# First layer of a two-layer attention kernel: the value product in four column quarters of 32 channels instead of two halves of 64

## The chip, the cores and the metric

The kernel runs on one core of one Trainium2 chip. The metric is the device time of one execution in microseconds (us), lower is better. TensorE (PE) does the matrix products, ScalarE (ACT) the exponentials and some copies, VectorE (DVE) maxima and small vector work, GpSimd (POOL) part of the sums, and SyncE (SP) starts the DMAs.

## The reference

Two self-attention layers over 8 images of 64x64 pixels with 64 channels, so 4096 tokens for each image. All is float32.

```
def layer0(x):                       # x: 8 images, xf = [8, 4096, 64]
    f, g, hh = xf @ wf + bf, xf @ wg + bg, xf @ wh + bh      # 8, 8 and 64 channels
    attn = softmax(einsum('bnk,bmk->bnm', g, f))
    return gamma * einsum('bnm,bmc->bnc', attn, hh) + x

def layer1(x):
    q, k, v = x @ Wq + bq, x @ Wk + bk, x @ Wv + bv          # 64 channels each
    attn = softmax(einsum('bic,bjc->bij', q, k))
    out = einsum('bmn,bmc->bnc', attn, v)                    # attention transposed
    return gamma * out + x
```

## The kernel before

The 8 images are worked one after the other, first layer and then second layer of each. What follows concerns the first layer.

The queries of an image are four chunks of 1024, and the keys are 32 tiles of 128. A chunk `q` is a loop of 32 steps `i` (`chunk0`), one for each key tile. The order on each engine is the order of the code; semaphores connect the engines. On TensorE a step is, in this order:

- `scores0` (L448): the scores of key tile `i` against the 1024 queries, as two matmuls of 512 columns in float16, with 34 of the 128 contraction rows. Between them stand two matmuls of the pass ahead (`max_pass_tiles`, L420), 33 contraction rows, which make scores of a later chunk only so that VectorE can take row maxima from them (`block_max`, L895). The L448 and L420 matmuls lie in different row groups of the array and all use its 128 columns.
- `values0` (L462), for the key tile four steps back (`LAG0`): it takes the exponentials `e_whole` (128 keys x 1024 queries, float32) and multiplies them with the value tile `proj[..., GFW:PW]` (128 keys x 64 channels). The 64 channels fill only half of the array's columns, so the first 512 queries go to columns 0 to 63 and the other 512 to columns 64 to 127. Both write bank 0 of `sum_banks`.
- `sum_of` (L484), every fourth step behind `values0`: it adds the exponentials over the keys for the softmax denominators. The other three of four key tiles are added up on GpSimd (`add_probs`, L346, L343) in `e_sum`. `sum_of` multiplies with a block of ones `ones_w` of 32 columns, in four column groups, each with its own quarter of 256 queries (`SUMS = 4`, `SQ = 256`), into bank 1.

ScalarE takes the exponential of each step's scores (L730), two steps behind at most. At the start of the next chunk the previous one is finished: values of its last four tiles in steps 0 to 3, `last_sums0` in step 4, VectorE's reciprocal of the sums (L900, `inv_d`), `spread0` (L494, two column groups of 64) in step 5, and VectorE's two products (L931, L932). The values of the new chunk are one step later than `LAG0` until step 8 (`CATCH_AT`), which does two value tiles, with a `sum_of` between them. Step 25 waits for VectorE's row maxima of the next chunk (L923), and step 26 (`MROW_AT`) transposes them (`max_rows`, L431, 34 columns) for ScalarE's copy L711, for which step 27 waits.

In the first chunk of an image (q = 0) there is no earlier chunk to finish, and values start in step 4. After the fourth chunk come the second layer's projections (L396) with the last value tiles between them.

The second layer's scores (L544) and values (L556) both use two column groups of 64 with all 128 rows.

A float32 matmul is two records in the trace, so 4096 records at L462 are 2048 matmuls, two for each of 1024 steps.

Of the kernel before, what the change touches and what calls it, by code (L numbers as in the profile page):

```python
# [24 lines left out]
P = 128  # L25
# [5 lines left out]
def attention_pair_kernel(nc, x, wf, bf, wg, bg, wh, bh, gamma0, wq, bq, wk, bk, wv, bv, gamma1, out):  # L31
    B, H, W, C = x.shape
# [13 lines left out]
    GFW = 2 * CK  # L46
    PW = GFW + C
# [20 lines left out]
    SUMS = 4  # L68
# [14 lines left out]
    with ExitStack() as ctx:  # L83
        def sb(name, shape, dt):
            return ctx.enter_context(nc.sbuf_tensor(name, shape, dt))
# [6 lines left out]
        sum_banks = ctx.enter_context(nc.psum_tensor("sum_banks", [P, 4, BANK], F32))  # L92
# [33 lines left out]
        proj = sb("proj", [P, 2, T, PW], F32)  # L126
# [77 lines left out]
        def on_pool(i):  # L204
            return i % GROUP != GROUP - 1
# [157 lines left out]
        def _(pe):  # L363
# [92 lines left out]
            def values0(image, par, q, i):  # L456

                pe.wait_ge(exp0_done, image * NCH * T + q * T + i + 1 + FREE_ST)
                if i == 0:
                    pe.wait_ge(v0_copied, image * NCH + q + FREE)  # L460
                for half in range(2):
                    mm = nc.tensor.matmul(sum_banks[half * C:(half + 1) * C, 0, :], proj[:, par, i, GFW:PW],  # L462
                                          e_whole[:, i % U0, half * BANK:(half + 1) * BANK], start=i == 0, stop=i == T - 1,
                                          skip_group_check=True)
                if i == T - 1:
                    mm.then_inc(v0_full, 1)
                    return
                if on_pool(i):
                    mm.then_inc(pv0_done, 1)
                    return  # L470
                if i == GROUP - 1:
                    pe.wait_ge(mid_ready, image * NCH + q + FREE)
                sum_of(e_whole[:, i % U0, :], i == GROUP - 1, False).then_inc(pv0_done, 1)
# [7 lines left out]
            def sum_of(terms, first, final):  # L481
                for c in range(SUMS):
                    rows = slice(c * (P // SUMS), (c + 1) * (P // SUMS))
                    mm = nc.tensor.matmul(sum_banks[rows, 1, 0:SQ], ones_w[:, :], terms[:, c * SQ:(c + 1) * SQ],  # L484
                                          start=first, stop=final, skip_group_check=True)
                return mm
# [16 lines left out]
            def chunk0(image, par, q):  # L503
# [5 lines left out]
                for i in range(T):  # L509
                    step = image * NCH * T + q * T + i  # L510
                    tiles = range(2 * (i % 4), 2 * (i % 4) + 2)
                    if q == 0 and i == 0:
                        pe.wait_ge(y_act, image * (NCH // 2) + FREE)
                        pe.wait_ge(y_dve, image * (NCH // 2) + FREE)
                    if i == MROW_AT + 1:
                        pe.wait_ge(mrow_sb, image * NCH + q + 2)
                    if i < LAST:
                        scores0(image, par, q, i, after(image, par, q + 1), EARLY + i // 4, tiles)
                    else:
                        scores0(image, par, q, i, after(image, par, q + 2), (i - LAST) // 4, tiles)  # L520
                    if i == MROW_AT:
                        max_rows(image, q)
                    if q == 0 or i > CATCH_AT:
                        if i >= LAG0:
                            values0(image, par, q, i - LAG0)
                    elif i < LAG0:
                        values0(image, par, q - 1, T - LAG0 + i)
                    elif i == LAG0:
                        last_sums0(image, q - 1)
                    else:  # L530
                        values0(image, par, q, i - LAG0 - DELAY)
                        if i == SPREAD_AT:
                            spread0(image, q - 1)
                        if i == CATCH_AT:
                            values0(image, par, q, i - LAG0)
# [608 lines left out]
```

## Time and profile before

| | |
|---|---|
| Median of 3 runs | 4095.75 us (4094.1 to 4095.97) |
| The profiled execution | 4098.83 us, its span 4097.0 us |
| PE busy | 3912.3 us (95%) |
| DVE busy | 3316.5 us (81%) |
| ACT busy | 2782.6 us (68%) |
| POOL busy | 1913.5 us (47%) |
| Mean granted TensorE clock | 0.979 |

The span is the time from the first to the last instruction. Busy shares are means over both layers. In the profile's lists "L462" is a line of the kernel, "out<-in" names what is written and read, "PE" are matmuls, "PEld" are weight loads, and "x4" counts the records. "128*64" is the part of the array that is used, rows times columns.

### The profile page before, as it was taken

The page shows a single profiled execution, that of the slowest core. Times are in us where ns is not written, and L with a number is a line of the kernel's source. Part 1 is how long each engine was busy: PE and PEld are TensorE (multiplying, and loading weights), DVE is VectorE, ACT ScalarE, POOL GpSimd, SP SyncE. Part 2 cuts the span into 40 slices and gives each one's busy share as a digit, 9 for nine tenths or more (in the row PEclk, how much of TensorE's full clock was granted, in tenths as well). Part 3 has the DMA queues.
Part 4 walks back from the last instruction along what each step waited for, and adds up shares of the span by engine and source line. Part 5 has one row for each costly group of instructions (what it writes and reads, how often), then busy time and mean ns, then how long its engine had stood idle before and what let it go on. Part 6 is the DMA issues. An engine that isn't in the chain of part 4 may idle for free.

```text
span 4097.0 us, 80148 instructions
## 1 busy us (share of the span) xinstructions
PE 3912.3 (95%) x25617; PEld 1432.4 (35%) x25617; DVE 3316.5 (81%) x6272; ACT 2782.6 (68%) x3610; POOL 1913.5 (47%) x876
## 2 busy tenths in 40 slices
PE   6999999999999999999999999999999999999999
PEld 3223442244422443224432244323442234422344
DVE  5777987788877888778877788777887779877798
ACT  1566776666766767666776667666676667766677
POOL 3695108931089311992039810497105961079410
PEclk8899999999999999999999999999999999999999
DMA  1000000000000000000000000000000000000000
GB/s 34 1 1 22 1 1 11 1 22 1 12 1 1 22 1 11 1 1 22 1 12 1 6 17 1 11 1 22 1 1 12 1 22 1 1 11 1 22 1 11
DMA packets 13900, 33.36 MB, mean 8 GB/s; under 512 B 3940, under 2 KB 3940, under 8 KB 12132
## 3 DMA queue, kind: packets, MB, share of 16 engines
q1 hardware_dynamic: 13540, 28.57, 2.4%
q8 instruction: 225, 3.69, 0.4%
q14 instruction: 135, 1.11, 0.1%
HBM read 11.78 MB, written 8.39 MB: 5 GB/s over the span
## 4 chain that ended last, share of the span: by engine, by line
PE 79%; DVE 11%; issue 7%; ACT 2%; DVEq 0%; SPq 0%; POOL 0%; DMA 0%; ACTq 0%; POOLq 0%
PE sum_banks L462 21%; PE score_banks L544 20%; PE sum_banks L556 19%; PE score_banks L448 11%; DVE tile_max L895 3%; PE sum_banks L484 3%; PE sum_banks L420 2%; DVE inv_d L900 1%; DVE e_whole L1062 1%; DVE c_stack L922 1%; PE sum_banks L494 1%; ACT g_tr L711 1%; DVE part_scr L1038 1%; PE score_banks L412 1%; DVE x_abs L876 0%
## 5 line engine op out<-in xcount | busy, mean ns | idle before, releaser
L895 DVE TENSOR_REDUCE tile_max<-sum_banks 128x1 f32<-128x512 f32 (+1 forms) x2128 | 1360.4, 684 | 474.1 <-PE sum_banks L420 471.7
L346 POOL TENSOR_TENSOR e_sum<-e_sum,e_whole 128x1024 f32<-128x1024 f32 x704 | 1660.1, 2358 | 129.9 <-ACT e_whole L730 82.1
L730 ACT ACTIVATE e_whole<-score_banks,no_bias,down 128x1024 f32<-128x1024 f32 x1024 | 1229.4, 1204 | 569.3 <-PE score_banks L448 532.6
L790 ACT ACTIVATE e_whole<-e_whole,exp_bias 128x1024 f32<-128x1024 f32 x1024 | 1176.2, 1149 | 514.9 <-DVE e_whole L1062 497.7
L1062 DVE TENSOR_SCALAR_CACHE_REDUCE e_whole<-score_banks,neg_down 128x1024 f32<-128x1024 f32 x1024 | 1293.6, 1281 | 121.8 <-PE score_banks L544 105.5
L462 PE MATMUL sum_banks<-e_whole,proj 128*64 128x512 f32 x4096 | 1122.5, 627 | 0.0
L556 PE MATMUL sum_banks<-e_whole,v_scaled 128*64 128x512 f32 x4096 | 1052.1, 594 | 40.1 <-DVE v_scaled L1051 29.0
L544 PE MATMUL score_banks<-k_high,q_split 128*64 128x512 f16 x4096 | 800.5, 381 | 12.3 <-DMA k_low<-k_low 9.7
L544 PE MATMUL score_banks<-k_low,q_split 128*64 128x512 f16 x4096 | 798.6, 380 | 0.0
L420 PE MATMUL sum_banks<-f_tr,g_tr 33*128 33x512 f16 x2128 | 700.0, 401 | 39.8 <-DVE tile_max L895 31.2
L448 PE MATMUL score_banks<-g_tr,f_tr 34*128 34x512 f16 x2048 | 648.3, 391 | 27.1 <-issue 11.2
L343 POOL TENSOR_TENSOR e_sum<-e_whole 128x1024 f32<-128x1024 f32 x32 | 75.4, 2356 | 1252.5 <-ACT e_whole L730 1252.5
L544 PEld LDWEIGHTS score_banks<-k_high,q_split 128*64 128x64 f16 x4096 | 244.7, 110 | 439.6 <-issue 169.9
L448 PEld LDWEIGHTS score_banks<-g_tr,f_tr 34*128 34x128 f16 x2048 | 123.2, 94 | 749.1 <-issue 596.8
L556 PEld LDWEIGHTS sum_banks<-e_whole,v_scaled 128*64 128x64 f32 x4096 | 299.2, 137 | 235.0 <-issue 43.4
L544 PEld LDWEIGHTS score_banks<-k_low,q_split 128*64 128x64 f16 x4096 | 246.5, 110 | 356.2 <-issue 250.3
L462 PEld LDWEIGHTS sum_banks<-e_whole,proj 128*64 128x64 f32 x4096 | 207.9, 136 | 303.9 <-issue 158.9
L420 PEld LDWEIGHTS sum_banks<-f_tr,g_tr 33*128 33x128 f16 x2128 | 177.5, 94 | 204.3 <-DVE tile_max L895 128.1
L790 ACT ACTIVATION_READ_ACCUMULATOR e_whole<-e_whole,exp_bias 128x1 f32 x1024 | 190.7, 186 | 0.0
L1051 DVE TENSOR_TENSOR v_scaled<-v,norm_w 128x256 f32<-128x256 f32 x256 | 115.2, 450 | 62.3 <-DVE norm_w L1042 60.1
L484 PE MATMUL sum_banks<-e_whole,ones_w 128*32 128x256 f32 x2048 | 164.5, 393 | 0.0
L317 POOL TENSOR_TENSOR f_stack<-fg_high,ones_h 128x512 f16<-128x512 f16 x20 | 20.9, 1062 | 253.4 <-issue 224.9
(128 smaller groups left out, 1735.5 us busy)
## 6 DMA issues: line engine op xcount, KB each, us to landing
x_in<-in_x_dram SPq DMA_DIRECT2D x11, 1024.0 KB, 5.1
out_dram<-y_out SPq DMA_DIRECT2D x32, 256.0 KB, 2.8
k_high<-k_high SPq DMA_DIRECT2D x32, 128.0 KB, 2.2
k_low<-k_low SPq DMA_DIRECT2D x32, 128.0 KB, 2.2
w<-in_L_conv_wg_dram SPq DMA_DIRECT2D x2, 2.0 KB
w<-in_L_conv_wf_dram SPq DMA_DIRECT2D x2, 2.0 KB
w<-in_L_conv_wh_dram SPq DMA_DIRECT2D x2, 16.0 KB
b<-in_L_conv_bh_dram SPq DMA_DIRECT2D x1, 32.0 KB
```

The costliest lines, as they stand in the source:

```text
L346: nc.gpsimd.tensor_tensor(acc, acc, e_whole[:, i % U0, :], ALU.add).then_inc(e_added, 1)
L420: nc.tensor.matmul(sum_banks[:, (2 + j % banks) % 4, :], g_tr[HIGH:KX, par, q * CH + blk * P:q * CH + (blk + 1) * P], f_tr[HIGH:KX, par, j ...
L448: mm = nc.tensor.matmul(score_banks[:, 2 * (i % 2) + h, :], f_tr[0:KM, par, i * P:(i + 1) * P], g_tr[0:KM, par, q * CH + h * BANK:q * CH + ...
L462: mm = nc.tensor.matmul(sum_banks[half * C:(half + 1) * C, 0, :], proj[:, par, i, GFW:PW], e_whole[:, i % U0, half * BANK:(half + 1) * BAN ...
L484: mm = nc.tensor.matmul(sum_banks[rows, 1, 0:SQ], ones_w[:, :], terms[:, c * SQ:(c + 1) * SQ], start=first, stop=final, skip_group_check=True)
L544: mm = nc.tensor.matmul(bank[c * C:(c + 1) * C, :], q_split[:, query_col(i) + c * C:query_col(i) + (c + 1) * C], k_part[:, col:col + BANK] ...
L556: mm = nc.tensor.matmul(sum_banks[half * C:(half + 1) * C, j, :], v_scaled[:, u // NCH, j, :], half_of_chunk(u, half), start=i == 0, stop= ...
L730: nc.scalar.activation(e_whole[:, i % U0, :].rearrange("p (a n) -> p a n", a=2), score_banks[:, 2 * (i % 2):2 * (i % 2) + 2, :], ACT.Exp, ...
L790: nc.scalar.activation(e_whole[:, u, :], e_whole[:, u, :], ACT.Exp, bias=exp_bias[:, u:u + 1], scale=-1.0, accum_out=part_sum[:, u // NCH, ...
L895: nc.vector.reduce_max(tile_max[:, blk, j:j + 1], sum_banks[:, (2 + j % banks) % 4, :], AX_X).then_inc(a_used, 1)
L1051: nc.vector.tensor_tensor(v_scaled[:, par, :, :], v1[:, i, :].unsqueeze(1).to_broadcast([P, NCH, C]), norm_w[:, par, :].unsqueeze(2).to_br ...
L1062: nc.vector.tensor_scalar(e_whole[:, u, :], score_banks[:, 2 * (u % 2):2 * (u % 2) + 2, :] .rearrange("p a n -> p (a n)"), neg_down[:, par ...
```

## The change

`values0` issues four matmuls instead of two. Each takes 32 of the 64 channels as its weights and one of the two query halves as its moving data: quarters 0 and 1 are the two channel halves for the first 512 queries, quarters 2 and 3 those for the other 512. They write the same elements of bank 0 as before. The division of the array into four column groups of 32 is the one that `sum_of` has. Streamed columns (512 each) and semaphores stay as they are.

```
@@ values0 @@
-                for half in range(2):
-                    mm = nc.tensor.matmul(sum_banks[half * C:(half + 1) * C, 0, :], proj[:, par, i, GFW:PW],
+                for c in range(SUMS):
+                    rows = slice(c * (P // SUMS), (c + 1) * (P // SUMS))
+                    half, part = c // 2, c % 2
+                    mm = nc.tensor.matmul(sum_banks[rows, 0, :],
+                                          proj[:, par, i, GFW + part * (C // 2):GFW + (part + 1) * (C // 2)],
                                           e_whole[:, i % U0, half * BANK:(half + 1) * BANK], start=i == 0, stop=i == T - 1,
                                           skip_group_check=True)
```

No instruction changes its place; lines behind L461 move down by 3 (L462 becomes L464, L484 becomes L487). Two places on TensorE show what now stands beside what. The first is the end of step 8 in a chunk after the first of its image (the values of tile 3, the sums, the values of tile 4). Before:

```order
L420 MATMUL sum_banks<-f_tr,g_tr 128x512
L462 MATMUL sum_banks<-e_whole,proj 64x512 x2
L484 MATMUL sum_banks<-e_whole,ones_w 32x256 x4
L462 MATMUL sum_banks<-e_whole,proj 64x512 x2
L446 REGISTER_ALU
```

The same rows of the changed kernel:

```order
L420 MATMUL sum_banks<-f_tr,g_tr 128x512
L464 MATMUL sum_banks<-e_whole,proj 32x512 x4
L487 MATMUL sum_banks<-e_whole,ones_w 32x256 x4
L464 MATMUL sum_banks<-e_whole,proj 32x512 x4
L446 REGISTER_ALU
```

The values now have the 32-column groups of the sums between them. The second place is step 5 of such a chunk, where `spread0` (64-column groups) follows the values. Before:

```order
L420 MATMUL sum_banks<-f_tr,g_tr 128x512
L462 MATMUL sum_banks<-e_whole,proj 64x512 x2
L494 MATMUL sum_banks<-inv_d,ident 64x256 x4
L446 REGISTER_ALU
L448 MATMUL score_banks<-g_tr,f_tr 128x512
```

And in the changed kernel:

```order
L420 MATMUL sum_banks<-f_tr,g_tr 128x512
L464 MATMUL sum_banks<-e_whole,proj 32x512 x4
L497 MATMUL sum_banks<-inv_d,ident 64x256 x4
L446 REGISTER_ALU
L448 MATMUL score_banks<-g_tr,f_tr 128x512
```

Here the two neighbours had the same column groups before and have different ones now.

## Rows read from the trace of the kernel before

**Rows 1.** The page: busy time, and the chain that ended last by line
```profile
PE 3912.3 (95%) x25617; PEld 1432.4 (35%) x25617; DVE 3316.5 (81%) x6272; ACT 2782.6 (68%) x3610; POOL 1913.5 (47%) x876
...
PE sum_banks L462 21%; PE score_banks L544 20%; PE sum_banks L556 19%; PE score_banks L448 11%; DVE tile_max L895 3%; PE sum_banks L484 3%; PE sum_banks L420 2%; DVE inv_d L900 1%; DVE e_whole L1062 1%; DVE c_stack L922 1%; PE sum_banks L494 1%; ACT g_tr L711 1%; DVE part_scr L1038 1%; PE score_banks L412 1%; DVE x_abs L876 0%
```

**Rows 2.** Timeline, PE, first layer, steps 15 to 17: start us, duration us
```profile
1266.34 1.08 PE L462 MATMUL sum_banks<-e_whole,proj 128*64 128x512 f32 x4
1267.34 0.64 PE L484 MATMUL sum_banks<-e_whole,ones_w 128*32 128x256 f32 x8
...
1267.92 0.39 PE L420 MATMUL sum_banks<-f_tr,g_tr 33*128 33x512 f16 x1
...
1268.45 1.08 PE L462 MATMUL sum_banks<-e_whole,proj 128*64 128x512 f32 x4
1269.46 0.39 PE L448 MATMUL score_banks<-g_tr,f_tr 34*128 34x512 f16 x1
...
1269.69 0.39 PE L420 MATMUL sum_banks<-f_tr,g_tr 33*128 33x512 f16 x1
```

**Rows 3.** Timeline, PE, second layer, where scores and values both have 64-column groups
```profile
1042.40 0.38 PE L544 MATMUL score_banks<-k_low,q_split 128*64 128x512 f16 x2
1042.62 1.02 PE L556 MATMUL sum_banks<-e_whole,v_scaled 128*64 128x512 f32 x4
1043.47 0.38 PE L544 MATMUL score_banks<-k_high,q_split 128*64 128x512 f16 x2
```

**Rows 4.** Groups by form, weight loads of one chunk: count, busy us, mean ns, idle
```profile
L462 PEld LDWEIGHTS sum_banks<-e_whole,proj 128*64 128x64 f32 x128 | 6.4, 134 | 8.8 <-ACT e_whole L730 4.7 <-issue 4.1
L484 PEld LDWEIGHTS sum_banks<-e_whole,ones_w 128*32 128x32 f32 x64 | 1.3, 108 | 5.9 <-issue 5.9
```

**Rows 5.** Timeline, PE, the first four records of one group of sums
```profile
1267.34 0.42 PE L484 MATMUL sum_banks<-e_whole,ones_w 128*32 128x256 f32 x4
```

**Rows 6.** Timeline, DVE, beside the steps of rows 2
```profile
1268.35 1.29 DVE L895 TENSOR_REDUCE tile_max<-sum_banks 128x1 f32<-128x512 f32 x2 [0.84 <-PE sum_banks L420]
```

**Rows 7.** Timeline, PE, step 8 of a chunk that finishes another
```profile
1253.01 0.39 PE L420 MATMUL sum_banks<-f_tr,g_tr 33*128 33x512 f16 x1 [0.21 <-DVE tile_max L895]
1253.33 1.08 PE L462 MATMUL sum_banks<-e_whole,proj 128*64 128x512 f32 x4
1254.34 0.64 PE L484 MATMUL sum_banks<-e_whole,ones_w 128*32 128x256 f32 x8
1254.90 1.08 PE L462 MATMUL sum_banks<-e_whole,proj 128*64 128x512 f32 x4
1255.92 0.39 PE L448 MATMUL score_banks<-g_tr,f_tr 34*128 34x512 f16 x1
```

**Rows 8.** Timeline, all engines, step 5 of that chunk
```profile
1246.29 1.08 PE L462 MATMUL sum_banks<-e_whole,proj 128*64 128x512 f32 x4
...
1247.69 1.08 PE L494 MATMUL sum_banks<-inv_d,ident 128*64 128x256 f32 x8 [0.32 <-DVE inv_d L900]
```

**Rows 9.** The waits, whole span: us in total, times, longest us
```profile
PEld sum_banks L494 <- DVE inv_d L900: 46.6, 32, 2.2
```

**Rows 10.** Timeline, all engines, steps 26 and 27
```profile
1286.01 0.57 PE L431 MATMUL score_banks<-ident_h,c_stack 128*34 128x128 f16 x7
...
1286.42 0.22 PE L431 MATMUL score_banks<-ident_h,c_stack 128*34 128x128 f16 x1
1286.47 1.02 PE L462 MATMUL sum_banks<-e_whole,proj 128*64 128x512 f32 x3
...
1287.73 0.39 PE L448 MATMUL score_banks<-g_tr,f_tr 34*128 34x512 f16 x1 [0.23 <-ACT g_tr L711]
```

**Rows 11.** Timeline, POOL, the first sum of the next chunk
```profile
1300.34 2.37 POOL L343 TENSOR_TENSOR e_sum<-e_whole 128x1024 f32<-128x1024 f32 x1 [0.64 <-ACT e_whole L730]
```

**Rows 12.** Windows, first chunks of two images: length, PE, PEld, DVE, ACT, POOL, PEclk
```profile
1116.60:1179.30 62.70, 60.77 (x306) 14.16 (x306) 43.30 (x67) 39.44 (x33) 51.72 (x22) 0.84 0.03 8
1616.20:1673.40 57.20, 54.85 (x304) 13.48 (x304) 43.09 (x67) 39.30 (x33) 51.28 (x22) 0.94 0.06 19
```

## The prediction

> **What bounds the kernel now.** The page comes first: TensorE is busy 95% of the span, and of the chain that ended last L462, the line that changes, holds 21% and its partner L484 3% [rows 1]. So a gain or loss of TensorE time at L462 can reach the end, if nothing else is equally late. The page can't say how long one value product occupies the array, since its records overlap. The timeline can, if one reads from the start of one group to the start of the next [rows 2]. The values take 1.01 us until the next scores start (1268.45 to 1269.46). Values with sums behind them take 1.58 (1266.34 to 1267.92), of which the sums are 0.58.
>
> How much of this is streaming? The second layer has values of the same size (four records, float32, 512 columns, groups of 64), between scores that use the same column groups. There it is 0.85 us from values to scores (1042.62 to 1043.47), and 0.22 from the last scores to the values: they follow each other without a gap [rows 3]. So 0.85 is the streaming, and 1.01 - 0.85 = 0.16 is lost in the first layer, where each neighbour divides the array otherwise: drain behind the group, and the first weight load, for which nothing runs as cover. The sums stream half as many columns, 0.43, and lose 0.58 - 0.43 = 0.15. The loss thus belongs to the change of division and not to the number of matmuls. By the Trainium skill (TensorEngine Tiling, Key Properties) changing the tiling mode drains TensorE while other tiles of the same mode run on; the rows agree, with 0.16 and 0.15 against nothing.
>
> **The change, part by part.**
>
> *Streaming.* The two quarters of a query half read the same exponentials, 512 columns each. All four must run at the same time, or the group doubles. The sums show four groups of 32 at once: eight records with a mean of about 0.4 in 0.58 [rows 2, 5]. The second layer shows two groups with the same moving data at once: two records in 0.22 (1042.40 to 1042.62) [rows 3]. I take 0.85 as before.
>
> *Starts and weight load.* In a group of sums the first four records span 0.42, one lasts some 0.40: three more starts cost 0.02 [rows 5]. The values would have two starts more, 0.014. A weight load of 32 columns has a mean of 108 ns against 134 for 64 [rows 4], so the exposed first one is 0.026 shorter. Together a value group between scores goes from 1.01 to 1.00: 0.012 saved. The loss of a 32-column group is then that of the sums, 0.15 instead of 0.16, as it should be.
>
> *Values and sums together.* They have the same division now, so I expect no loss between them: 0.85 + 0.43 + 0.15 = 1.43 instead of 1.58, 0.155 saved (with the third decimals of the means). Bounds: 0.012 if the gap between them stays, 0.155 if it goes.
>
> *Step 8.* Values, sums and values follow each other, 1253.33 to 1255.92, 2.59 us [rows 7]. New: 0.85 + 0.43 + 0.85 + 0.15 = 2.28, 0.31 saved.
>
> *New changes of division.* Two neighbours that agreed no longer do. `spread0` follows the values in step 5. The values end streaming near 1246.29 + 1.00 = 1247.29, drain included; L494 starts at 1247.69, because it waits for VectorE's reciprocal [rows 8]. So 0.40 covers it, and it waits so all 32 times [rows 9]. Without that cover it would cost 0.15 a time, 5 us in all. In step 26 the transposed maxima L431 use 34 columns of a 64-wide group and the values follow inside their stream; they would start about 0.13 later. The last pass starts near 1286.90, streams 0.43 and drains 0.10: 1287.43, or 1287.56 then. Step 27 waits until 1287.73 for ScalarE's copy [rows 10]. Hidden, at most 4 us if it were not.
>
> *What of it is on the path.* In chunks that finish another one, steps 5 to 7 lead through VectorE (reciprocal, two products, late maxima: L420 waits for them in step 8 [rows 7, 8]), step 24 through VectorE's maxima, step 26 through ScalarE's copy. Value time saved there is lost. The last four value tiles of an image lie beside ScalarE's and VectorE's work on the projections, before the same wait of L494 [rows 9]; I count nothing there. On the path remain: step 8 in 24 chunks; values with sums in six steps of those and seven of each first chunk, 24 x 6 + 8 x 7 = 200; values alone in 19 steps of those and 18 of each first chunk, 24 x 19 + 8 x 18 = 600.
>
> *VectorE is nearly as late.* Its two maxima start 0.43 after the first L420 of a step (1267.92 to 1268.35) and end 1.29 later, at 1269.64 [rows 2, 6]. The second L420 of the next step needs one of their banks and starts at 1269.69, 0.05 later, the time a semaphore takes, and its place in TensorE's own order is the same 1269.69 (0.23 behind the first) [rows 2]. So the two loops tie within 0.01. If values get 0.012 shorter, VectorE delays that L420 by 0.01 in every second step; the step after a delayed one has slack again. I give values alone 0.008 instead of 0.012, and values with sums 0.145 instead of 0.155. The sums' steps have slack on VectorE: it is idle 0.84 before the maxima there [rows 6].
>
> *GpSimd.* A chunk gets about 1.3 us shorter; GpSimd has 0.64 idle at its start [rows 11] and falls behind by under 1 us. Its last sum of a chunk ends at 1300.34 - 0.64 = 1299.70, before the exponential of the next chunk's step 1, and is wanted in step 4, three steps later; ScalarE needs the exponentials' slots only eight steps later. No cost.
>
> Sum: 24 x 0.31 = 7.4; 200 x 0.145 = 29.0; 600 x 0.008 = 4.8; together 41.2 us. The profiled execution would go from 4098.8 to 4057.6, its span from 4097.0 to 4055.8. It is 3.1 us above the median of the runs, so in medians: 4095.75 - 41.2 = 4054.5.
>
> *The clock.* TensorE starts an image's first chunk partly at 1.2 GHz, after little work: of two such chunks one has a mean granted clock of 0.84 and takes 62.7, the other 0.94 and 57.2 [rows 12]. How long it stays low differs from image to image, so a shift of everything in time deals these 5.5 us anew, eight times. I take 0 and allow 10 to both sides.
>
> **Rivals.**
>
> *A: the gap between values and sums stays* (because it comes from the other bank, the other weights or the last weight load, not from the division). Against it: in the second layer neighbours with other banks and other weights leave no gap [rows 3]. Then only 0.012 a group: 848 groups x 0.008 = 7, 4089.
>
> *B: VectorE or GpSimd takes more.* Both are near. If each plain step gives nothing and values with sums half, 7.4 + 200 x 0.08 = 23, 4072.
>
> *C, slower: four more records cost issue time in each group.* The nearest row is L431, where passes follow each other every (0.57 - 0.22) / 6 = 0.058 us [rows 10], though each also streams 128 columns, so it is an upper bound; the lower is the 0.007 from the starts [rows 5]. At 0.058, four more cost 0.23 in each of the 200 + 600 + 48 = 848 groups on the path: 196, minus 36 for the gaps, 4256. It decides from 36 / 848 = 0.043 a group, 0.011 a record. Against it: the sums issue eight records with the same 0.15 of loss as the values' four. The Trainium skill says (TensorEngine Tiling, Instruction Overhead) that each matmul has about 60 cycles of overhead. As an estimate by that page, four more at 2.4 GHz are 0.1 us a group, 85 in all, which less 36 would be 4145; the rows of the sums speak against it.
>
> *D, much slower: the four don't run at once*, since two groups with the same data and two with other data at 512 columns is not what either row shows alone. Twice the streaming: 848 x 0.85 = 720, 4780.
>
> **How the numbers follow.** Forecast 0.78, A 0.07, B 0.08, C 0.04, D 0.03. The likeliest gives 4054.5. Without VectorE's tie it would be 200 x 0.155 + 600 x 0.012 + 7.4 = 46, 4050; with nothing from the plain steps 36, 4059; the clock adds 8 to both. That makes 4042 to 4067, and to take in most of B I go to 4072. A measurement of this kernel tells a difference from about 0.2% (8 us). A lies at 7, so of its 0.07 some 0.04 go to no change. Faster 0.89, same 0.04, slower 0.07.
>
> **What would show it.** In the profile after, a value group should hold eight records at 128*32, start to start 1.00 to the scores and 0.85 to the sums; values with sums 1.43 and step 8's three groups 2.28. The first L420 after a plain step should be on time, and every second one should wait about 0.01 for VectorE. L494 should still start on VectorE's reciprocal, and step 27 on ScalarE's copy. POOL's idle time at a chunk's start should shrink. Eight records in 1.7 us would be D, a group of about 1.1 C, 1.00 between values and sums A. The prediction goes wrong above all if the array handles two column groups of 32 inside one half otherwise than the sums' four, or if the granted clock falls more often.

## The result and the profile after

| | before | after |
|---|---|---|
| Median of 18 runs | 4097.89 us (4092.91 to 4110.02) | 4089.47 us (4085.45 to 4097.8) |
| Ratio, 95% interval | | 0.998 (0.9972 to 0.9987) |
| The profiled execution's span | 4097.0 us | 4091.7 us |
| Mean granted TensorE clock | 0.979 | 0.973 |

The changed kernel is faster by 0.2%, 8 us by the medians. The forecast was 4054.5 (4042 to 4072), 41 us less than before. So four fifths of the forecast gain are missing.

First the page after: busy times, and the chain that ended last by line.

```profile
PE 3888.8 (95%) x29713; PEld 1422.4 (35%) x29713; DVE 3332.5 (81%) x6272; ACT 2782.5 (68%) x3610; POOL 1917.6 (47%) x876
...
PE sum_banks L464 21%; PE score_banks L547 20%; PE sum_banks L559 20%; PE score_banks L448 11%; DVE tile_max L898 4%; PE sum_banks L420 2%; PE sum_banks L487 2%; DVE inv_d L903 1%; DVE e_whole L1065 1%; DVE c_stack L925 1%; DVE part_scr L1041 1%; PE sum_banks L497 1%; ACT g_tr L714 1%; PE score_banks L412 1%; DVE x_abs L879 1%
```

Against [rows 1] TensorE has lost 24 us of busy time, but the span only 5. VectorE has gained 16 us, though its instructions are the same. That is the first sign of where the time went. Next the steps themselves: the timeline of PE, values alone, then values with sums.

```profile
1269.08 1.06 PE L464 MATMUL sum_banks<-e_whole,proj 128*32 128x512 f32 x8
1270.08 0.39 PE L448 MATMUL score_banks<-g_tr,f_tr 34*128 34x512 f16 x1
1270.08 0.39 PE L420 MATMUL sum_banks<-f_tr,g_tr 33*128 33x512 f16 x1
...
1270.63 1.06 PE L464 MATMUL sum_banks<-e_whole,proj 128*32 128x512 f32 x8
1271.52 0.61 PE L487 MATMUL sum_banks<-e_whole,ones_w 128*32 128x256 f32 x8
1272.06 0.39 PE L448 MATMUL score_banks<-g_tr,f_tr 34*128 34x512 f16 x1
```

Values alone take 1.00 us until the scores (1.01 in [rows 2]), with sums 1.43 instead of 1.58. The next timeline is PE in step 8 of a chunk that finishes another, where 1244.87 to 1247.16 is 2.29 us instead of the 2.59 of [rows 7].

```profile
1244.87 1.07 PE L464 MATMUL sum_banks<-e_whole,proj 128*32 128x512 f32 x8
1245.75 0.61 PE L487 MATMUL sum_banks<-e_whole,ones_w 128*32 128x256 f32 x8
1246.18 1.04 PE L464 MATMUL sum_banks<-e_whole,proj 128*32 128x512 f32 x8
1247.16 0.39 PE L448 MATMUL score_banks<-g_tr,f_tr 34*128 34x512 f16 x1
```

The lengths of all three are as forecast; only inside them the sums start 0.88 to 0.89 behind the values, where 0.85 was expected, and what follows them comes that much sooner. So the gain was made, and given back elsewhere. To find the place, the starts of the first score matmul (L448) of all 1024 steps were read from both traces and the lengths added up, in us:

| | before | after | change |
|---|---|---|---|
| Start, up to the first step | 124.3 | 123.5 | -0.8 |
| 8 first chunks without steps 25 and 26 | 429.7 | 417.7 | -12.0 |
| 24 later chunks without step 25 | 1333.2 | 1303.1 | -30.1 |
| Steps 25 and 26 of the first chunks | 43.5 | 58.4 | +14.9 |
| Step 25 of the later chunks | 58.9 | 72.1 | +13.2 |
| Rest: last step of the layer, projections, second layer, end | 2107.4 | 2116.9 | +9.5 |
| Span | 4097.0 | 4091.7 | -5.3 |

The second and third row, nearly the steps on which the forecast rests, gave 42.1 us, where 41.2 were worked out. Step 25, and the clock that falls behind it, took 28 back, and code that is the same in both kernels 9.5.

How much of this is the clock? Each trace also lists the stretches in which TensorE was granted 1.2 GHz instead of 2.4. Where TensorE is always busy, such a stretch costs about half its length, an estimate that two profiled executions of one kernel bear out below (e5 and e5_again). In the row of the rest these stretches add up to 15.0 us before and 34.1 after: half the difference is 9.5, the whole of that row. In the second row they are 5 us shorter after, so some 3 of the 42.1 us are luck. Steps 25 and 26 of the one first chunk in which the clock did not fall after the change take 3.47 and 2.25 us, against 2.98 and 2.25 before: so about 4 of the 14.9 us are a longer wait, eight times 0.49, and 11 the clock. The waits thus took 13.2 + 4 = 17 us back, and the clock, 11 and 9.5 less the 3, some 18.

What happens before step 25? The first view is the timeline of DVE in steps 24 and 25 of the kernel before, the next that of GpSimd beside it.

```profile
1281.10 0.22 DVE L921 TENSOR_REDUCE row_max<-tile_max 128x8 f32<-128x64 f32 x1
1281.36 1.32 DVE L922 TENSOR_SCALAR c_stack<-row_max 128x8 f16<-128x8 f32 x1
1282.70 0.20 DVE L923 SCALAR_TENSOR_TENSOR c_stack<-row_max,c_stack 128x8 f16<-128x8 f32 x1
```

```profile
1280.27 2.36 POOL L346 TENSOR_TENSOR e_sum<-e_sum,e_whole 128x1024 f32<-128x1024 f32 x1
```

An operation on 8 elements (`c_high` in `split_max`) lasts 1.32 us. It ends at 1282.68, 0.05 behind the end of GpSimd's running add (1280.27 + 2.36 = 1282.63). The same two views of the changed kernel:

```profile
1271.83 0.22 DVE L924 TENSOR_REDUCE row_max<-tile_max 128x8 f32<-128x64 f32 x1
1272.09 1.73 DVE L925 TENSOR_SCALAR c_stack<-row_max 128x8 f16<-128x8 f32 x1
1273.85 0.19 DVE L926 SCALAR_TENSOR_TENSOR c_stack<-row_max,c_stack 128x8 f16<-128x8 f32 x1
1273.95 1.29 DVE L898 TENSOR_REDUCE tile_max<-sum_banks 128x1 f32<-128x512 f32 x2
```

```profile
1271.40 2.37 POOL L346 TENSOR_TENSOR e_sum<-e_sum,e_whole 128x1024 f32<-128x1024 f32 x1
```

Now it lasts 1.73, again until GpSimd's add is over (1273.77). What sets the end of this add? GpSimd's timeline has its last pause of a chunk in step 13. The add behind that pause is, before and after:

```profile
1263.22 2.35 POOL L346 TENSOR_TENSOR e_sum<-e_sum,e_whole 128x1024 f32<-128x1024 f32 x1 [0.51 <-ACT e_whole L730]
```

```profile
1254.30 2.38 POOL L346 TENSOR_TENSOR e_sum<-e_sum,e_whole 128x1024 f32<-128x1024 f32 x1 [0.33 <-ACT e_whole L733]
```

From there eight adds follow each other without a pause. Their row ends 19.41 us later before (1263.22 to 1282.63) and 19.47 later after (1254.30 to 1273.77). It did not get shorter with TensorE's steps. VectorE is there earlier, waits longer, and its late maxima hold TensorE in step 25. From step 13 to step 24 such a chunk got 0.49 us shorter and step 25 0.55 longer.

In the first chunks of images GpSimd's row begins in step 9 already and has eleven adds, 26.7 us before and 26.8 after. There the kernel before waited in `c_high` too, 1.82 to 1.86 us. DVE and GpSimd:

```profile
1161.82 1.86 DVE L922 TENSOR_SCALAR c_stack<-row_max 128x8 f16<-128x8 f32 x1
1163.72 0.19 DVE L923 SCALAR_TENSOR_TENSOR c_stack<-row_max,c_stack 128x8 f16<-128x8 f32 x1
```

```profile
1161.28 2.36 POOL L346 TENSOR_TENSOR e_sum<-e_sum,e_whole 128x1024 f32<-128x1024 f32 x1
```

In the changed kernel another operation waits there:

```profile
1154.17 0.19 DVE L925 TENSOR_SCALAR c_stack<-row_max 128x8 f16<-128x8 f32 x1
1154.39 2.22 DVE L926 SCALAR_TENSOR_TENSOR c_stack<-row_max,c_stack 128x8 f16<-128x8 f32 x1
```

```profile
1154.21 2.36 POOL L346 TENSOR_TENSOR e_sum<-e_sum,e_whole 128x1024 f32<-128x1024 f32 x1
```

L925 (`c_high`) started in the 0.04 us before the add of 1154.21 and took 0.19. L926 (`c_low`), which reads two tensors in SBUF, then took 2.22 us and was done 0.04 behind that add's end. Where the one operation gets through, the next pays for nearly a whole add. It is the same, eleventh add of the row whose end held `c_high` before. By windows over steps 24 to 26 of this chunk (length, PE, PEld, DVE, ACT, POOL, PEclk):

```profile
1154.10:1155.70 1.60, 1.60 (x17) 0.29 (x13) 1.53 (x3) 0.83 (x1) 1.52 (x2) 1.00 0.04 10
1155.70:1159.80 4.10, 2.72 (x16) 0.42 (x12) 3.29 (x5) 1.58 (x2) 3.94 (x3) 0.83 0.00 0
1159.80:1163.60 3.80, 3.70 (x32) 1.39 (x32) 1.45 (x3) 1.69 (x2) 3.72 (x2) 0.73 0.00 0
```

TensorE is busy 2.72 of 4.10 us in step 25, and the granted clock falls to its lower level in this step and the next (means of 0.83 and 0.73). In seven of the eight first chunks a stretch at 1.2 GHz starts there; before it was one of eight. In the 24 later chunks, whose step 25 takes 3.00 us, none does.

### The profile page after: what moved, and what is told of

Read it like the earlier page. It is cut to its first block, busy times and chain, and to the rows that moved or that the text cites. A ratio compares the mean times of both kernels' runs of the same rounds, so it can differ in the third digit from the quotient of the medians.

```text
span 4091.7 us, 88340 instructions
## 1 busy us (share of the span) xinstructions
PE 3888.8 (95%) x29713; PEld 1422.4 (35%) x29713; DVE 3332.5 (81%) x6272; ACT 2782.5 (68%) x3610; POOL 1917.6 (47%) x876
## 4 chain that ended last, share of the span: by engine, by line
PE 79%; DVE 11%; issue 7%; ACT 2%; DVEq 0%; SPq 0%; POOL 0%; DMA 0%; ACTq 0%; POOLq 0%
PE sum_banks L464 21%; PE score_banks L547 20%; PE sum_banks L559 20%; PE score_banks L448 11%; DVE tile_max L898 4%; PE sum_banks L420 2%; PE sum_banks L487 2%; DVE inv_d L903 1%; DVE e_whole L1065 1%; DVE c_stack L925 1%; DVE part_scr L1041 1%; PE sum_banks L497 1%; ACT g_tr L714 1%; PE score_banks L412 1%; DVE x_abs L879 1%
## 5 line engine op out<-in xcount | busy, mean ns | idle before, releaser
L464 PE MATMUL sum_banks<-e_whole,proj 128*32 128x512 f32 x8192 | 1111.2, 616 | 0.0
L448 PE MATMUL score_banks<-g_tr,f_tr 34*128 34x512 f16 x2048 | 650.3, 392 | 21.7 <-issue 10.6
L448 PEld LDWEIGHTS score_banks<-g_tr,f_tr 34*128 34x128 f16 x2048 | 123.0, 94 | 769.7 <-issue 614.9
L464 PEld LDWEIGHTS sum_banks<-e_whole,proj 128*32 128x32 f32 x8192 | 166.5, 109 | 303.3 <-issue 151.6
L487 PE MATMUL sum_banks<-e_whole,ones_w 128*32 128x256 f32 x2048 | 158.4, 381 | 0.0
```

Of the source, the lines that this page charges most:

```text
L448: mm = nc.tensor.matmul(score_banks[:, 2 * (i % 2) + h, :], f_tr[0:KM, par, i * P:(i + 1) * P], g_tr[0:KM, par, q * CH + h * BANK:q * CH + ...
L464: mm = nc.tensor.matmul(sum_banks[rows, 0, :], proj[:, par, i, GFW + part * (C // 2):GFW + (part + 1) * (C // 2)], e_whole[:, i % U0, half ...
```

## The experiments

Two theories stood at first. Theory 1: what is missing waits at step 24 for GpSimd, and the clock falls because TensorE idles there. Theory 2: the clock falls more often for another reason and is itself the loss. The medians below stand beside a median of the kernel before from the same chip: 4101.24 for the first four kernels, 4095.53 for e5 to e7, 4094.59 for the last three. All kernels from e1 on leave out `c_low`, the low half of the softmax shift; it cancels in the softmax. Medians from different chips are best compared by their ratios.

**e1_after_no_port**: the changed kernel with (beside it the number of linked operations, `LINK_MAX`, goes from 2 to 1)

```
-                c_high, c_low = c_stack[:, place % 2, :, KS], c_stack[:, place % 2, :, KS + 1]
-                chain.link(nc.vector.tensor_scalar(c_high, row_max0[:, :], -2.0 ** -MAX_UP, None, ALU.mult))
-                nc.vector.scalar_tensor_tensor(c_low, row_max0[:, :], -2.0 ** -MAX_UP, c_high,
-                                               ALU.mult, ALU.subtract).then_inc(max_split, 1)
+                c_high = c_stack[:, place % 2, :, KS]
+                nc.vector.tensor_scalar(c_high, row_max0[:, :], -2.0 ** -MAX_UP, None, ALU.mult, ALU.min,
+                                        accum_out=max_rest[:, 0:1]).then_inc(max_split, 1)
```

> The changed kernel; VectorE's c_high is made by a tensor_scalar that also writes an accumulator (as L1062 does), and c_low, the low half of the softmax shift, is left out and stays zero (the shift cancels in the softmax). Theory 1 (the lost gain waits at step 24 on GpSimd): in the changed kernel VectorE's small op of 8 elements takes 1.72 us in later chunks because it starts only when GpSimd's running add ends, and in first chunks the next op, with two SBUF inputs, takes 2.2 us. Neither op should wait now: c_high near 0.2 us, step 25 falls from 3.01 to about 1.6 us in 24 chunks (-34 us), in the 8 first chunks from about 4.1 to 1.6 and step 26 from about 3.3 to 2.25 (-28 us), the time is about 4027 us (4020 to 4040), and the extra stretches at half clock in steps 25 and 26 vanish. Theory 2 (the clock falls for another reason, about 50 us more at half speed than before, 26 us of time): the stretches stay and the time is 4050 or more. Theory 3 (GpSimd's adds bound the chunk at 23 x 2.44 = 56.2 us): chunks stop at 56.2 us and part of the gain goes into ScalarE's waits for the adds.

**e2_before_no_port**: the same edit on the kernel before.

> The kernel before with the same edit of c_high and c_low (the low half of the softmax shift is left out). Theory 1: VectorE waited for GpSimd here too, 1.3 us for 8 elements; step 25 falls from 2.45 to about 1.6 us in later chunks (-21 us) and from 2.98 in first chunks (-11 us): about 4065 us. The distance to e1_after_no_port is then what the column quarters are worth with nothing else late: 24 x 0.31 + 200 x 0.145 + 600 x 0.008 = 41 us by my sum. Theory 2: the distance stays near the 8 us measured between the two kernels.

Measured: e1 4035.35 us, ratio 0.9842 (0.9829 to 0.9855); e2 4051.31, ratio 0.9888 (0.9873 to 0.9903). The duration of L925 in e1, its 33 times, min/median/max ns:

```profile
L925 DVE TENSOR_SCALAR_CACHE_REDUCE c_stack<-row_max x33: 187/189/192, 111.0 to 3754.7; 128x8 f16<-128x8 f32 x33
```

and in the changed kernel without the edit:

```profile
L925 DVE TENSOR_SCALAR c_stack<-row_max x33: 184/1718/1740, 110.8 to 3810.1; 128x8 f16<-128x8 f32 x33
...
L926 DVE SCALAR_TENSOR_TENSOR c_stack<-row_max,c_stack x33: 194/195/2254, 111.0 to 3811.8; 128x8 f16<-128x8 f32 x33
```

The wait is gone, and with it step 25: 1.56 us in every chunk of both kernels, instead of 2.45 and 3.00 in the later chunks. So theory 1 holds for its first half: 4035 against 4027 expected, and 54 us below the changed kernel (1.4% by the ratios). e2 is a miss: 4065 was expected, and 16 us between the two are nearer to the 8 of theory 2 than to the 41 of theory 1. Theory 3's bound is not reached: a later chunk takes 56.53 us, and GpSimd's adds don't stop it.

With the wait gone on both sides, the later chunks can be compared for what the quarters are worth. Added up from the traces, they take 1371.0 us in e2 (24 chunks, the last of an image to its step 31) and 1340.7 in e1: 30.3 less. By my terms it is 24 x 0.31 + 136 x 0.145 + 456 x 0.008 = 30.8 (eight of the 144 steps with sums are last steps, which fall under the rest). Yet the medians are only 16 apart, and the two profiled executions 7. The rest (the row of that name above) takes 2101.2 us in e2 and 2127.2 in e1, with the same code, and the mean granted clock is 0.984 in e2 and 0.974 in e1. That is 2 x 0.010 x 4040 = 81 us more at the lower level. Of these 54.5 lie in the rest, and half of them is 27 us, the 26 of the rest. Outside the start, whose length did not follow the clock (123.1 to 124.3 us in the twelve profiled executions, with 58 to 108 us at the lower level), e1 has 141.0 us at the lower level and e2 72.7. With half of each taken off, the two executions are 41.3 us apart, where the sum gave 41.2. That is an estimate, and the closeness is partly luck.

The second half of theory 1, that the extra stretches at half clock would vanish, is only half right: they vanished in steps 25 and 26 and came up in the second layer.

**e4_no_low_part**: as e1, but `c_high` by the old instruction.

> The changed kernel with c_low left out alone; c_high is made by the old tensor_scalar. Theory 1 says two different ops wait for GpSimd: in the later chunks the tensor_scalar still waits 1.7 us (saved only 0.24 us a chunk, 6 us in all), in the first chunks the op that waited 2.2 us is gone, and with it the clock's fall in step 26 (about -26 us): about 4058 us. If only the tensor_scalar is the cause, about 4083.

Measured: 4062.2 us, ratio 0.9909 (0.9894 to 0.9924), 4058 expected. Step 25 of the first chunks fell from 31.7 us in all eight to 12.6 (`c_high` takes 0.19 there); that of the 24 later ones only from 72.1 to 68.0, since L925 still takes 1.72 at the median there. So two operations wait for GpSimd, each in its own chunks.

**e3_quarters_at_sums**: as e1, with quarters only where the values stand beside sums:

```
+                parts = 2 if i % GROUP == GROUP - 1 and i < T - 1 or (q > 0 and i == GROUP) else 1
+                for c in range(2 * parts):
+                    half, part = c // parts, c % parts
```

> As e1_after_no_port, but quarters only for the value groups that stand beside sums (every fourth tile, and tile 4 behind them in step 8); all others in two halves. If the gain is the gap between values and sums, almost all of it stays: e1 plus 600 x 0.008 = 5 us, about 4032. If the gain is in each group (weight loads), most of it goes: nearer to e2_before_no_port.

Measured: 4032.44 us, ratio 0.9829 (0.9814 to 0.9844), not different from e1's. A later chunk takes 56.62 us against 56.53 in e1 and 57.83 in e2. So 1.21 of the 1.30 us of a chunk come from the eight groups beside sums: the gap between values and sums is the gain, and the shorter weight load in the other groups is worth next to nothing.

**The stretches in the second layer.** One of e1's that repeats stands behind an operation of VectorE on 4 elements. Timelines of e1, DVE, GpSimd and PE:

```profile
923.96 4.15 DVE L1040 CUSTOM_DVE_ANT_0 part_scr<-part_sum,chunk_w 128x4 f32<-128x4 f32 x1
```

```profile
923.52 4.57 POOL L326 TENSOR_TENSOR proj<-proj,b 128x2048 f32<-128x2048 f32 x1
```

```profile
925.77 0.38 PE L547 MATMUL score_banks<-k_low,q_split 128*64 128x512 f16 x2
929.10 1.20 PE L559 MATMUL sum_banks<-e_whole,v_scaled 128*64 128x512 f32 x4 [2.95 <-DVE v_scaled L1053]
930.30 0.64 PE L547 MATMUL score_banks<-k_high,q_split 128*64 128x512 f16 x2
930.73 0.64 PE L547 MATMUL score_banks<-k_low,q_split 128*64 128x512 f16 x2
```

It is the same wait: L1040 reads two tensors and ends with GpSimd's `bias_h` of 4.57 us. TensorE idles 2.95 us, and its next matmuls last 0.64 instead of 0.38, at half clock. In e2 the same wait is split in two in seven of eight images, 0.8 and 3.15 us, because of how VectorE and GpSimd happen to meet; no stretch at half clock follows there. But the whole wait is not needed for one: e1 has a stretch there in all eight images, also in the one where the wait is split.

**e5_after_pieces**, **e6_before_pieces**, **e7_sums_pieces** (their expectations follow in this order): e1, e2 and e3 with `bias_h` and `bias_v` in pieces of 512 elements. Of the edit only the new lines of `bias_h` are shown; those of `bias_v` are alike, and the waits for both count the pieces:

```
+                for n in range(PIECES):
+                    h = proj[:, par, n * (T // PIECES):(n + 1) * (T // PIECES), GFW:PW]
+                    nc.gpsimd.tensor_tensor(h, h, b0[:, GFW:PW].unsqueeze(1).to_broadcast([P, T // PIECES, C]), ALU.add
+                                            ).then_inc(h_biased, 1)
```

> As e1_after_no_port (column quarters, VectorE's c_high and c_low without waits for GpSimd; the low part of the softmax shift is left out), and GpSimd's bias additions in the second layer in four pieces each (bias_h 4 x 512 elements instead of one instruction of 4.57 us, bias_v 2 x 512 for each half). In e1 VectorE's op of 4 elements at L1040 takes 4.15 us once per image in 7 of 8 images while bias_h runs, and TensorE is idle 2.9 us there, after which the granted clock is at half for 3.4 us. Theory 1 (the same wait for GpSimd, only elsewhere; the clock falls because TensorE idles long): L1040 takes at most about 1.3 us, the stretch at half clock behind it vanishes, each image gains 2 to 4 us: 4035 - 24 = 4011. Theory 2 (the clock falls for another reason): the stretches stay, and only the wait's 2 to 3 us an image go, or nothing.

> The same two edits on the kernel before (column halves; the low part of the softmax shift is left out). In e2 the wait was split in two, 0.8 and 3.15 us, with no fall of the clock behind it: it should gain less than e5, about 16 us: 4035. The distance to e5 then comes nearer to the 41 us that the step lengths give (16 us between e1 and e2): about 24 to 40 us by theory 1, 16 by theory 2.

> As e5_after_pieces with quarters only for the value groups beside sums, as in e3_quarters_at_sums (the low part of the softmax shift is left out). Its step lengths gave 56.62 us a later chunk against 56.53 for quarters everywhere; so it should be equal to e5 within 5 us if nothing else differs.

Measured: e5 4016.01 us, ratio 0.981 (0.9797 to 0.9824); e6 4053.11, ratio 0.9898 (0.9883 to 0.9913); e7 4020.15, ratio 0.9813 (0.98 to 0.9826). The operation of 4 elements in e5, min/median/max ns of 256:

```profile
L1043 DVE CUSTOM_DVE_ANT_0 part_scr<-part_sum,chunk_w x256: 157/159/1133, 376.2 to 4004.2; 128x4 f32<-128x4 f32 x128
```

The longest wait is now 1.13 us. The stretches at half clock at this place became rare: 31 in the 48 images of the six kernels with `bias_h` in one piece, 8 in the 48 of the six executions with pieces. e5 is faster than e1 by 0.003 (about 13 us; 24 were expected), e6 is not faster than e2, where 16 were expected: a miss. The step lengths repeat (e6 to e5: 30.6 us in the later chunks). The distance between the two is now 37 us, near the 41 of the sum (42.4 in the profiled executions, with half of the lower level taken off as above). Part of this agreement is luck with the clock, as the next runs show.

**e8_last_tiles_halves**, **e9_last_tiles_only**, **e5_again**: in e5's trace the clock was at half for 6.8 us from the end of the first layer in six of eight images (the expectation says five), behind a pause of TensorE that is 0.16 us longer with quarters. The edits are the conditions `q < NCH - 1 or i < T - LAG0` (e8) and `q == NCH - 1 and i >= T - LAG0` (e9) for quarters.

> As e5_after_pieces (quarters; the low part of the softmax shift is left out), but the last four value tiles of an image, which lie beside the second layer's projections, stay in halves. In e5 quarters finish there earlier without use: TensorE idles 1.58 us in front of L497 instead of 1.42, and in five of eight images the granted clock is at half for 6.8 us from there; in e6 and e7, with halves there, it never is. If the longer pause is the cause, these stretches vanish, 5 x 3.4 = 17 us at most: about 4003 us. If it is chance of position, the time stays at 4016, with as many stretches at half clock here or elsewhere.

> The opposite: halves as in e6_before_pieces everywhere, quarters in the last four value tiles of an image alone (the low part of the softmax shift is left out). If the longer pause is the cause, stretches at half clock appear at the layer's end in most images and the time is some 10 us above e6's 4053, about 4063. If it is chance of position, 4053 within 5.

> The same kernel as e5_after_pieces once more, beside the two others on one chip (the low part of the softmax shift is left out): 4016 within 5 us. It shows how far the place of the stretches at half clock repeats from one execution to another.

Measured: e8 4016.81 us, ratio 0.9812 (0.9799 to 0.9825); e9 4058.57, ratio 0.991 (0.9895 to 0.9925); e5_again 4017.89, ratio 0.9816 (0.9803 to 0.9829). e8 gains nothing against e5. And the same kernel a second time had its stretches at half clock elsewhere: the rest took 2114.0 us in the first profiled execution and 2100.9 in the second, the first chunks 442.0 and 449.0. Both follow the clock: the lower level has 26.7 us less in the rest and 13.6 more in the first chunks, and half of each is 13.4 and 6.8, for 13.1 and 7.0 measured. e9 against e6 is 0.0012 slower, within the intervals, and lies halfway between its two expected times: inconclusive.

The places of the stretches say more than the times. In e9, with quarters in the last four tiles alone, the clock was at half behind that pause in four of eight images, where e6 had none. The first of them by windows:

```profile
365.40:372.20 6.80, 6.80 (x40) 3.61 (x40) 3.40 (x5) 1.53 (x2) 2.49 (x2) 0.50 0.17 39
```

Over all twelve profiled executions such a stretch stands there in 16 of 48 images where the last tiles are in quarters (1, 4, 0, 6, 1 and 4 for the changed kernel, e1, e4, e5, e5_again and e9), and in 1 of 48 where they are in halves (e8). So the pause of 1.58 instead of 1.42 us goes together with a fall of the clock, though not in each execution: six against one in the same kernel. Quarters there gained nothing, and by half of its length each such stretch costs 3.4 us; in the medians this can't be told from noise.

## Why the prediction was wrong

*Right: what the array does.* Four quarters run at once; values and sums follow each other with at most 0.04 us between them (0.89 from values to sums where 0.85 is streaming, 0.54 from there to the scores); 1.00, 1.43 and 2.29 us were measured for 1.00, 1.43 and 2.28. The tie with VectorE is there too: plain steps alternate between 1.534 and 1.559 us where it was 1.547 and 1.558, so the second of a pair gained nothing. Rivals A, C and D fell. `spread0` still waits for the reciprocal (0.33 us in the changed kernel, [rows 8] had 0.32), and step 27 for ScalarE's copy: step 26 takes 2.25 us in the later chunks of both. (Its working there takes 0.10 us of drain, which no run shows by itself.) GpSimd's idle time at the start of the chunk of [rows 11] shrank from 0.64 to 0.25 us, as forecast.

*Wrong: the step on GpSimd, "No cost", and with it what of step 24 is on the path.* I asked only whether GpSimd's results come late for those that wait for them by a semaphore, and they don't. VectorE waits for GpSimd without a semaphore: `c_high` and `c_low` did not get through while an add ran that had begun before them. I saw step 24 lead "through VectorE's maxima" and counted it as lost, one step of 0.012. But the end of that wait is an end of a GpSimd add, in a row of adds that runs since step 13, in the first chunks since step 9. So nothing that TensorE saved between 13 and 24 could come through, 0.49 us a chunk, and in the first chunks it was the same, whichever of the two operations waited. Against the sum of 41.2 stand 13.2 and about 4 us of wait, and about 11 for the clock that fell behind it.

The wait was in the trace of before, 1.32 us for 8 elements, as a row that I read and didn't ask about. The Trainium skill states it (SBUF — State Buffer, Who interferes with whom): VectorE and GpSimd share one pair of ports under an exclusive lock. `tensor_scalar` in a two-port mode, and operations with two SBUF inputs against a GpSimd instruction that reads SBUF, wait until the running instruction is over; the form that also writes an accumulator does not enter these modes. The runs agree with all three: 1.72 us for `c_high`, 2.22 for `c_low` behind the start of an add, 0.19 for the form with an accumulator.

*Mis-sized: the clock.* I allowed 10 us (and put only 8 into the range), for the first chunks alone; it took some 18 in the profiled executions. The changed kernel has a mean clock of 0.973 there against 0.979, which is 2 x 0.006 x 4092 = 49 us more at half speed. It is not these two executions alone: the 18 of the changed kernel have 0.967 to 0.974, mean 0.971, and the 29 of the kernel before that stand beside the experiments 0.972 to 0.980, mean 0.976. In steps 25 and 26 this follows TensorE's pause; that the pause is its cause is borne out by e1 and e4, where pause and stretches vanish together in the first chunks. The other +9.5 us in unchanged code are stretches at the lower level too. Most stand behind the wait for `bias_h`, in seven of eight images after the change and three before; the wait is in one piece of 4.1 us in six of eight images after and in one before, but stretches follow split waits as well, so that this decides it is not shown. Why the clock falls behind one pause and not behind an equal one stays open, and so does all but the layer's end (e9) of why e1 had more such stretches than e2. Two executions of one kernel differ by 13 us in one part, so the distances of 16 and 37 us between the pairs e2, e1 and e6, e5 don't measure the change better than to some 15 us. The lengths of the steps in the later chunks do: 30.3 us of 30.8. So do whole executions, as an estimate, once half of their time at the lower level is taken off: 41.3 and 42.4 us of 41.2.

*Rival B* (VectorE or GpSimd takes more) was the nearest, but with another mechanism and 4072: it took the two engines' loads for the danger, not the tie between them.

The best version is e5: quarters, `c_high` without the lock, and `bias_h` in pieces, 4016 us, 1.9% below the kernel before; part of this is the work that is left out with `c_low`. e7 and e8 are equal to it within the intervals.

## What to carry to other kernels

Put a small group of matmuls into the column division of its neighbour: here that gave 0.14 to 0.15 us for each boundary that vanished, and the size of the weights hardly mattered.

Before a gain on one engine is counted, look for small VectorE operations that last far longer than their size explains and end together with a GpSimd instruction. They tie VectorE to GpSimd without a semaphore, and whatever is saved since GpSimd's last idle time ends in that wait. Use a form that doesn't need the shared port, and cut long GpSimd instructions into pieces.

When code that was not changed takes longer, look at the granted clock by stage, and profile the kernel twice before a cause is sought in the change.

## What was not expected of the hardware

An operation on 8 elements took 0.19, 1.32, 1.73, 1.86 or, for its neighbour, 2.22 us, by its place against GpSimd's adds alone. When VectorE had waited for the end of an add, GpSimd's next add did not hold it up, though it is recorded from the same moment as `c_low` (1273.85 in the chunk above): in all 32 chunks before and the 24 later ones after, `c_high` and then `c_low` went through there (`c_low` in 0.19 to 0.20 us). Only where `c_high` met the gap of 0.08 us between two adds did `c_low` have to wait. For the pair it makes little difference: it was done 0.04 us behind the end of the add where `c_low` waited, and 0.27 behind it where `c_high` did. What counts is which add it meets.

After a pause of 2.95 us TensorE's next matmuls ran at half clock in e1, and after pauses of 1.3 and 1.9 us at the same place in e2 they did not. Nor did they behind the one pause of e2 that was as long, in the fourth image. The timeline of PE in e2, and the window around it (length, PE, PEld, DVE, ACT, POOL, PEclk):

```profile
1914.33 1.08 PE L556 MATMUL sum_banks<-e_whole,v_scaled 128*64 128x512 f32 x4 [2.94 <-DVE v_scaled L1050]
```

```profile
1913.00:1918.00 5.00, 3.55 (x24) 1.37 (x26) 4.64 (x11) 2.49 (x5) 0.32 (x1) 1.00 0.01 2
```

The same pause, with the granted clock at 1.00 throughout: its length alone doesn't decide.
